# Attention pair: one reciprocal per unit on packed denominators, spread by DMA, and the final step moved to VectorE

## The reference

```python
h = group_norm(x)                       # 32 groups, per image
q, k, v = h @ Wq + bq, h @ Wk + bk, h @ Wv + bv
attn = softmax(q @ k.T * C ** -0.5)     # 1024 x 1024 per image
x = x + (attn @ v) @ Wo + bo
```

## Time and profile before

| | us |
|---|---|
| three runs: median (lowest to highest) | 239.01 (236.49 to 240.69) |
| the profiled execution: its own time | 236.29 |
| its span, first to last instruction | 234.3 |
| PE busy | 199.0 (85%) |
| POOL busy | 151.0 (64%) |
| DVE busy | 135.0 (58%) |
| ACT busy | 101.5 (43%) |

### The profile page before, as it was taken

The page is one execution under the profiler, slowest core; times in us unless marked ns, Lnnn a source line. Parts: engine busy times, 40 slices in busy tenths (PEclk is TensorE's granted clock), DMA queues, the critical chain, the costliest instruction groups (busy, mean ns, idle before and its releaser), DMA issues.

```text
span 234.3 us, 3189 instructions
## 1 busy us (share of the span) xinstructions
PE 199.0 (85%) x1216; PEld 106.0 (45%) x1216; DVE 135.0 (58%) x184; ACT 101.5 (43%) x136; POOL 151.0 (64%) x93
## 2 busy tenths in 40 slices
PE   8868467999999499994999599986999979949980
PEld 7654334455555244543455255444545434514420
DVE  1558962657687445856388357926588639005343
ACT  3422303744657036550574338531556444434610
POOL 1200001979688944699386958697487979997905
PEclk9995757999999958998899999997999999999998
DMA  7150320140041000500014000500032100010011
GB/s 225 48 134 0 76 59 1 36 101 1 0 93 46 0 3 0 134 1 4 0 27 107 1 3 0 134 4 0 0 73 66 45 1 0 4 45 0 0 45 45
DMA packets 4718, 9.14 MB, mean 39 GB/s; under 512 B 800, under 2 KB 1760, under 8 KB 4704
## 3 DMA queue, kind: packets, MB, share of 16 engines
q1 hardware_dynamic: 4272, 8.42, 14.1%
q10 hardware_dynamic: 432, 0.53, 0.6%
HBM read 1.58 MB, written 1.05 MB: 11 GB/s over the span
## 4 chain that ended last, share of the span: by engine, by line
PE 53%; POOL 20%; issue 8%; DVE 7%; ACT 4%; POOLq 0%
PE ps_attn L614 14%; POOL prob_sum L235 12%; PE ps_max L574 6%; PE ps_scores L594 5%; DVE neg_max L426 4%; PE ps_scores L596 4%; PE ps_scores L602 4%; PE ps_scores L598 4%; PE ps_misc L564 4%; PE ps_scores L556 3%; POOL attn L241 3%; POOL xs L244 3%; ACT probs L327 3%; PE ps_misc L621 3%; DVE stats L380 1%
## 5 line engine op out<-in xcount | busy, mean ns | idle before, releaser
L235 POOL TENSOR_TENSOR prob_sum<-prob_sum,probs 128x1024 f32<-128x1024 f32 x44 | 104.3, 2371 | 22.6 <-ACT probs L327 19.0
L426 DVE TENSOR_REDUCE neg_max<-ps_max 128x1 f32<-128x1024 f32 x59 | 72.1, 1222 | 42.5 <-PE ps_max L575 42.3
L327 ACT ACTIVATE probs<-ps_scores 128x1024 f32<-128x1024 f32 x64 | 62.8, 1023 | 71.6 <-PE ps_scores L603 71.3
L614 PE MATMUL ps_attn<-probs,vals 128*64 128x512 f32 x256 | 63.8, 619 | 0.0
L574 PE MATMUL ps_max<-keys,q_hi 64*128 64x512 f32 x59 | 28.6, 485 | 16.3 <-DVE neg_max L426 16.3
L224 POOL TENSOR_TENSOR rstd<-var_eps,minus_half 128x1 f32<-128x1 f32 x8 | 4.4, 549 | 51.3 <-DVE var_eps L396 51.3
L434 DVE RECIPROCAL rden<-den 128x128 f32<-128x128 f32 x28 | 26.0, 938 | 12.7 <-ACT den L333 12.7
L614 PEld LDWEIGHTS ps_attn<-probs,vals 128*64 128x64 f32 x256 | 15.9, 138 | 29.0 <-issue 20.1
L575 PE MATMUL ps_max<-keys,q_hi 64*128 64x512 f32 x59 | 28.7, 486 | 0.0
L574 PEld LDWEIGHTS ps_max<-keys,q_hi 64*128 64x128 f32 x59 | 11.3, 192 | 36.4 <-DVE neg_max L426 21.6
L594 PE MATMUL ps_scores<-q_hi,keys 64*128 64x512 f32 x64 | 27.2, 425 | 0.0
(11 more groups left out here) (78 smaller groups left out, 310.5 us busy)
## 6 DMA issues: line engine op xcount, KB each, us to landing
keys<-keys SPq DMA_DIRECT2D x16, 256.0 KB, 3.4
q_hi<-q_hi SPq DMA_DIRECT2D x16, 128.0 KB, 2.3
xs<-x_dram SPq DMA_DIRECT2D x4, 256.0 KB, 4.3
out_dram<-xs SPq DMA_DIRECT2D x3, 256.0 KB, 2.0
layer<-layers_dram ACTq DMA_DIRECT2D x2, 194.5 KB, 4.5
q_row<-max_rows SPq DMA_DIRECT2D x16, 2.0 KB
out_dram<-xs SPq DMA_DIRECT2D x4, 64.0 KB, 1.6
const_sb<-consts_dram ACTq DMA_DIRECT2D x1, 128.0 KB, 3.6
```

The lines of the kernel that those rows point to most:

```text
L235: pool.tensor_tensor(prob_sum[u % 2][:, :], first[:, :], probs[t][:, :], ALU.add).then_inc(added, 1)
L327: act.activation(probs[t][:, :], ps_scores[t % 2][:, :], ACT.Exp, scale=SCALE).then_inc(exp_done, 1)
L426: dve.tensor_reduce(neg_max[u % 2][:, t:t + 1], ps[:, :], AX.X, ALU.max, negate=True).then_inc(max_done, 1)
L614: mm = pe.matmul(ps_attn[half * C:(half + 1) * C, :], v, probs[t][:, cols], start=(t == 0), stop=(t == TILES - 1))
```

## The change

The denominator matmuls use a new constant, `chunk_ones`, which sends the sums of column chunk c (of four, 128 columns each) to output rows c, c + 4, c + 8 and so on. So a unit's 512 sums of a half lie as 64 rows of 128 columns, each value in 16 rows, and one reciprocal of 128 x 128, read straight from `ps_misc`, covers them; `copy_den` is gone. Four DMAs on SP (`spread_rden`) spread the result to the full `rden` of 128 x 512.

`finish` moves from POOL (between additions 5 and 6) to DVE (after the four row maxima at a window's end, and ahead of `gn_own`). The denominators' matmuls move from behind `values(w - 1, 7)` to behind `values(w, 1)`. `scores(w, 0)` now stands ahead of the group mean, `row_max(w + 2, 1)` ahead of `finish` and `gn_own`. In the last window three late additions on DVE take in all of tiles 4 to 7; two steps of denominator matmuls, both ahead of the last values, replace three; and POOL and DVE share the four chunks of the last `finish`. At the start POOL fills `chunk_ones`, and PE waits for it.

```diff
+            def spread_rden(u):
+                sp.wait_ge(rden_done, u + 1)
+                if u:
+                    sp.wait_ge(normed, u)
+                rows = rden_chunks[:, :]
+                for i in range(CHUNKS):
+                    to = rden[i::CHUNKS, :].rearrange("a (j n) -> a j n", j=CHUNKS)
+                    sp.dma_start(to, rows).then_inc(rden_spread, 16)
...
+            def store_last(image):
...
+                for c in range(CHUNKS):
+                    sp.wait_ge(last_final[c % 2], c // 2 + 1)
...
                     swap_q(w + 2)
                     swap_k(w + 2)
+                if w:
+                    spread_rden(w - 1)
                 if w + 1 < UNITS:
                     place_rows(w + 1)
                 if w > B:
-                    store(w - 1 - B, 1)
-            store(B - 1, CHUNKS)
+                    store(w - 1 - B)
...
+            pool.memset(chunk_ones[:, :], 0.0).then_inc(chunks_zero, 1)
+            pool.wait_ge(chunks_zero, 1)
+            for c in range(CHUNKS):
+                picked = chunk_ones[:, c * C:(c + 1) * C].rearrange("p (a j) -> p j a", j=CHUNKS)[:, c, :]
+                pool.memset(picked, 1.0).then_inc(chunks_set, 1)
...
-            def finish(u):
-                pool.wait_ge(rden_done, CHUNKS * (u + 1))
...
+            def finish_last():
+                a = attn[LAST % 2]
+                at = (LAST + B) * HALF
+                pool.wait_ge(attn_copied, UNITS)
+                pool.wait_ge(x_biased, UNITS)
+                for n, c in enumerate((0, 2)):
+                    pool.wait_ge(last_rden, c + 1)
+                    pool.tensor_tensor(a[:, cols], a[:, cols], rden[:, cols], ALU.mult).then_inc(last_normed[0], 1)
+                    pool.wait_ge(last_normed[0], n + 1)
+                                       xs[:, LAST * HALF + cols.start:LAST * HALF + cols.stop],
+                                       ALU.add).then_inc(last_final[0], 1)
...
                 for t in range(1, TILES if w < LAST else EARLY):
-                    if t == 6 and w:
-                        finish(w - 1)
                     add(w, t)
-                if w == LAST:
-                    finish(w - 1)
-            pool.wait_ge(x_biased, UNITS)
-            finish_last(LAST)
+            finish_last()
...
-            def copy_den(u):
-                act.wait_ge(den_mm, u + 1)
-                if u:
-                    act.wait_ge(rden_done, CHUNKS * u)
-                act.activation(den[:, :], ps_misc[:, :], ACT.Copy).then_inc(den_copied, 1)
...
-            def reciprocal(u, c):
-                if c == 0:
-                    dve.wait_ge(den_copied, u + 1)
-                    if u:
-                        dve.wait_ge(normed, u)
-                dve.reciprocal(rden[:, chunk(c)], den[:, chunk(c)]).then_inc(rden_done, 1)
+            def reciprocal(u):
+                dve.wait_ge(den_mm, u + 1)
+                if u:
+                    dve.wait_ge(rden_spread, 16 * CHUNKS * u)
+                dve.reciprocal(rden_chunks[:, :], ps_misc[:, 0:HALF // CHUNKS]).then_inc(rden_done, 1)
+
+            def finish(u):
+                a = attn[u % 2]
+                dve.wait_ge(attn_copied, u + 1)
+                dve.wait_ge(rden_spread, 16 * CHUNKS * (u + 1))
+                dve.tensor_tensor(a[:, :], a[:, :], rden[:, :], ALU.mult).then_inc(normed, 1)
+                dve.wait_ge(normed, u + 1)
+                dve.wait_ge(x_biased, u + 1)
+                dve.tensor_tensor(xs[:, slot(u + B)], a[:, :], xs[:, slot(u)], ALU.add).then_inc(final_done, 1)
+
+            def reciprocal_last():
+                dve.wait_ge(normed, LAST)
+                dve.wait_ge(den_mm, UNITS)
+                for c in range(CHUNKS):
+                    dve.reciprocal(rden[:, chunk(c)], ps_misc[:, chunk(c)]).then_inc(last_rden, 1)
+
+            def finish_last():
...
+                for n, c in enumerate((1, 3)):
+                    cols = chunk(c)
+                    dve.wait_ge(last_rden, c + 1)
+                    dve.tensor_tensor(a[:, cols], a[:, cols], rden[:, cols], ALU.mult).then_inc(last_normed[1], 1)
+                    dve.wait_ge(last_normed[1], n + 1)
+                    dve.tensor_tensor(xs[:, at + cols.start:at + cols.stop], a[:, cols],
+                                      xs[:, LAST * HALF + cols.start:LAST * HALF + cols.stop],
+                                      ALU.add).then_inc(last_final[1], 1)
...
-                if w:
-                    reciprocal(w - 1, 0)
-                if nxt:
                     row_max(w + 1, 5)
                 if prep:
                     low_q(w + 2)
                     low_k(w + 2)
                 if w:
-                    reciprocal(w - 1, 1)
+                    reciprocal(w - 1)
                 if nxt:
                     row_max(w + 1, 6)
+                    row_max(w + 1, 7)
+                if prep:
+                    row_max(w + 2, 0)
+                    row_max(w + 2, 1)
                 if w:
-                    reciprocal(w - 1, 2)
-                if nxt:
-                    row_max(w + 1, 7)
-                if w:
-                    reciprocal(w - 1, 3)
-                if prep:
-                    row_max(w + 2, 0)
+                    finish(w - 1)
                 if w + 3 < UNITS:
                     if w + 3 >= B:
                         dve.wait_ge(final_done, w + 3 - B + 1)
                     gn_own(w + 3)
-                if prep:
-                    row_max(w + 2, 1)
                 if w == LAST:
-                    for t in range(EARLY + 1, TILES - 1):
+                    for t in range(EARLY + 1, TILES):
                         add_late(t)
-            dve.wait_ge(normed, LAST)
-            dve.wait_ge(den_mm, UNITS)
-            for c in range(CHUNKS):
-                dve.reciprocal(rden[:, chunk(c)], ps_misc[:, chunk(c)]).then_inc(rden_done, 1)
+            reciprocal_last()
+            finish_last()
...
-                for half, cols in enumerate(halves()):
-                    mm = pe.matmul(ps_misc[half * C:(half + 1) * C, :], ones[:, :], prob_sum[u % 2][:, cols],
-                                   start=True, stop=True)
+                n = HALF // CHUNKS
+                for c in range(CHUNKS):
+                    for half in range(2):
+                        mm = pe.matmul(ps_misc[half * C:(half + 1) * C, 0:n], chunk_ones[:, c * C:(c + 1) * C],
+                                       prob_sum[u % 2][:, half * HALF + c * n:half * HALF + (c + 1) * n],
+                                       start=(c == 0), stop=(c == CHUNKS - 1))
...
-                    pe.wait_ge(den_copied, LAST)
+                    pe.wait_ge(rden_done, LAST)
                     pe.wait_ge(added, ADDS * LAST + EARLY - 1)
-                elif part == 1:
-                    pe.wait_ge(late_added, TILES - EARLY - 2)
                 else:
-                    pe.wait_ge(exp_done, TILES * UNITS)
-                summed = (prob_sum[LAST % 2], LATE, probs[TILES - 1])[part]
+                    pe.wait_ge(late_added, TILES - EARLY - 1)
+                summed = (prob_sum[LAST % 2], LATE)[part]
...
+            pe.wait_ge(chunks_set, CHUNKS)
...
                 next_max(2)
+                scores(w, 0)
                 if prep:
                     pe.wait_ge(max_staged, w + 1)
                     group_mean_of(w + 2)
-                scores(w, 0)
                 if w == 0:
                     pe.wait_ge(max_done, TILES + 2)
                 scores(w, 1)
...
                 if w:
                     values(w - 1, 6)
                     values(w - 1, 7)
-                    if prep:
-                        pe.wait_ge(var_ready, w + 3)
-                    else:
-                        pe.wait_ge(max_staged, min(w + 1, UNITS))
-                    denominators(w - 1)
                 next_max(4)
                 scores(w, 2)
                 scores(w, 3)
...
                 if prep:
                     pe.wait_ge(exp_done, TILES * w + 3)
                     project(w + 2)
-                    if w:
-                        pe.wait_ge(den_copied, w)
+                    pe.wait_ge(var_ready, w + 3)
                     project_v(w + 2)
                 values(w, 0)
                 values(w, 1)
+                if w:
+                    if prep:
+                        pe.wait_ge(v_copied, w + 3)
+                    else:
+                        pe.wait_ge(max_staged, min(w + 1, UNITS))
+                    denominators(w - 1)
                 next_max(6)
                 if prep:
                     pe.wait_ge(q_lo_done, w + 3)
...
                 values(w, 2)
                 values(w, 3)
                 if nxt:
-                    if prep:
+                    if w:
+                        pe.wait_ge(rden_done, w)
+                    else:
                         pe.wait_ge(v_copied, w + 3)
-                    elif w:
-                        pe.wait_ge(den_copied, w)
```

(23 more changed lines are left out.)

33 lines of the change are left out of this document (14 added, 19 removed).

## The result

The changed kernel took 250.22 us (median of 4 runs, 249.27 to 251.15), the kernel before 239.85 (4 runs, 236.49 to 241.78): ratio 1.0525, 95% interval 1.0408 to 1.0641. It is slower. The forecast was 243 us, no change to speak of, with a range from 222 to 249.

The account below looks back on a forecast made before the run. PE, busy 85% of the span, was taken to bound most of it. Windows +7.4, window 6 +2.0, window 7 and tail -2.75, clock +0.4 on a 234.3 us span gave 241.35, with 2.0 around it 243 us; range 222 to 249.

Parts of the forecast that it names:

- The mechanism of finish on DVE: `finish` at a window's end: multiplication waits for POOL's addition 6, addition for addition 7; about 1.2 + 0.7 and 2.4 + 0.7 us.
- The first two rivals: DVE and POOL don't lock: 219.4 us, chance 0.1; they lock, but `finish` fits between additions 6 and 7: 225, chance 0.18.
- The body of a window: Group mean to group mean at full clock: 13.6 us ahead of exp 4, 13.15 after, 26.75 instead of 24.92.
- The spread and the denominators: Four DMAs on SP land before `finish` asks, except in window 7; sixteen denominator steps take 1.1 us.
- Window 6, window 7 and the tail: Window 6 gets 2.0 us longer; window 7 and the tail together change by -2.75 us.
- The price of the clock: After PE's idle stretches: four of 3.9 us cost about 6 us, window 6 about 0.7; 0.4 more than before.
- the third rival: PE's longer idle stretch costs the clock each time and twice as long, 12.8 us instead of 6: 250 us, chance 0.12.
- The start: POOL's five memsets delay PE's warm-up matmuls about 1 us, covered by the load of x; under 1 us if not.
- The profiled execution was 2.7 below the median of the runs shown; I don't add that: Kernel before: the 2.7 us was left out of the forecast, as part of it is luck with the clock.

Follow-up runs that it names:

- warm_gap: The changed kernel with 28 unread matmuls on PE ahead of the group mean in windows 2 to 5; 237.13 us, ratio 0.9882.
- warm_all: The changed kernel with the `chunk_ones` wait moved to the first denominators and PE's idle stretches at the start and in windows 2 to 6 filled with unread matmuls; 228.91 us.
- before_finish_dve: The kernel before with `finish` alone moved to DVE; 241.24 us, ratio 1.0076.
- half_adds: The changed kernel with POOL's additions 6 and 7 of units 0 to 6 each cut into two of 128 x 512; 234.23 us, ratio 0.968.
- before_order: The kernel before with `row_max(w + 2, 1)` ahead of `gn_own` and `scores(w, 0)` ahead of the group mean, nothing else; 224.31 us, ratio 0.9334.

## Why the prediction was wrong

*The mechanism of finish on DVE: right.* I wrote that the multiplication waits for addition 6, holds addition 7 back, and the addition waits for addition 7, at about 1.2 + 0.7 and 2.4 + 0.7 us, with PE idle for 3.9 us. Measured: 2.07 and 2.72, and 3.84 to 3.87. Only what I had POOL lose was too much: its addition 7 was longer by 0.24 us, not 0.65. Taking POOL's last additions away or moving `finish` undid the wait, and halving them made it shorter. The first two rivals, 219 and 225 us, fell with that.

*The body of a window: 0.8 us too long.* I had 26.75 us from mean to mean at full clock; warm_gap shows 25.92: 13.1 instead of 13.6 ahead of exp 4 and 12.83 instead of 13.15 behind it.

*The spread and the denominators: right but for window 6.* Four DMAs were issued in 2.5 us and landed 1.9 us after issue, ahead of DVE's request in windows 1 to 5; `finish` waited for them in window 7, 4.0 us, and in window 6, 1.06 us, which I had not seen. The sixteen steps took 0.88 us, not 1.1.

*Window 6, window 7 and the tail: right in sum.* From the group mean of window 5 (174.81) to the end it was 73.6 us; my marks give 73.5, with some 2.3 us of clock in them. At full clock (warm_all, 156.41 to 225.9) this part took 69.5, so by that estimate the clock cost about 4 of the 73.6 and the rest of my marks was 1.7 too long. That the two cancel is luck.

*The price of the clock: the first failed term.* "Four of 3.9 us at the same price cost about 6", 1.6 each. It is the third rival that came in, to which I gave 0.12: the longer idle stretch costs the clock each time and for longer. From the mean of window 2 (87.08) to that of window 5 (174.81) it was 87.7 us, 3.3 a period above warm_gap's 25.92; my sum had 3 x 26.75 and 1.5 each for the clock, 84.75. Of the 3 us between the two, the clock makes 5.5 (3.3 instead of 1.5, three times) and the body, 0.8 too long each time, takes 2.5 back. That the rival's 250 us were met so closely is luck: it lacks the 3.9 us of the two terms below, and the body and the last windows took as much back. I had named the point from which this rival decides, PE idle for more than 3.1 us, had forecast 3.9, and still priced it by the average over the old ones. Why it costs more here isn't settled. Its length alone doesn't say: before_finish_dve had stretches as long and kept more of its clock behind three of four, half_adds had them at 1.72 us and lost nearly as much behind three of four in its profiled execution. What the change and half_adds share is their order: PE stops behind one score tile. The traces record no other pause of PE above 0.06 us around these waits, so what it is in the order that does it is not shown.

*The start: the second.* I took the load of x for the cover of about 1 us of delay. The load doesn't cover the warm-up matmuls, which last until the data is there: `own` was ready at 5.04 us, and PE took it at 6.48, behind them. The delay came through whole, 1.3 us in the trace and 1.4 between the medians.

*"The profiled execution was 2.7 below the median of the runs shown; I don't add that": the third.* It should have been added. In the stretch from 18 to 50 us the profiled execution of before had a granted clock of 0.74, the change 0.63, and so had before_order, whose start is that of the kernel before:

```profile
18.00:50.00 32.00, 25.19 (x117) 14.69 (x118) 20.55 (x30) 10.23 (x15) 8.14 (x5) 0.63 0.18 40
```

The trace that I built on had drawn a lucky start, worth some 2.5 us, which no other profiled execution shows (0.57 or 0.63, and 1.00 where the start was filled). That it is luck and not the order of this kernel is seen from its other executions, whose mean clock was as low as 0.904 against the 0.932 of the profiled one. The three terms, about 3, 1.4 and 2.5 us, make up the 7 us between the forecast span of 241.35 and the measured 248.4.

*What I didn't see at all:* that the order alone, with `finish` left where it was, is worth 16 us. I had its terms (1.2 us of row maximum behind `gn_own`, 0.9 of scores ahead of the mean) but only used them to size the change.

## What to carry to other kernels

Before moving a two-input SBUF operation between VectorE and GpSimd, look at what the other engine runs at that time: each waits for the other's whole instruction, and in a chain of two dependent operations the other engine's next one gets in between. Where a wait can't be removed, ask first which independent step is queued behind the late result or ahead of it; moving that may give more than making the late step faster. Price an idle stretch of TensorE with the clock that it costs afterwards, take the dearest case that the trace shows rather than the mean, and build the sum on the median run and not on a lucky profile.

## What was unexpected of the hardware

Unread matmuls in the idle stretches bought 13 us at 3.9 us of idle time in four places, and 7.5 us at 0.3 to 2.8 us of it in six places at the start (218.55 to 211.09), where the clock over 18 to 50 us went from 0.57 to 1.00. Idle stretches of 0.6 to 0.8 us between windows lowered it in no trace here. What an idle stretch does to the clock doesn't follow from its length alone: of the 7 us behind 3.84 us of idle time in the old order about half were at the lower level three times and all once; behind 3.87 us in the new order nearly all, four times; behind 1.72 us in the new order most, three times, and half once, in one execution whose clock was lower than that of the others of its kernel.
